# Four-layer block on one core: 23 expert tiles for 24, the last expert's constant row from DVE and one product, constant products moved and added on PE

## The reference

```
logits = _gelu(x @ rw1) @ rw2
wgt, idx = jax.lax.top_k(jax.nn.softmax(logits, axis=-1), TOP_K)   # TOP_K = 2
for e in range(E):                                                 # E = 8
    Ye = _gelu(x @ w1[e] + b1[e]) @ w2[e] + b2[e]
    Ce = _gelu(b1[e]) @ w2[e] + b2[e]
    for k in range(TOP_K):
        mask = idx[..., k] == e
        active = jnp.any(mask).astype(x.dtype)
        out = out + active * wgt[..., k:k + 1] * jnp.where(mask[..., None], Ye, Ce)
```

## Time and profile before

| | us |
|---|---|
| median of 3 runs | 454.55 |
| the three runs | 454.42, 454.55, 456.42 |
| the profiled execution, its own time | 456.11 |
| its span, first to last instruction | 454.3 |
| PE busy | 387.2 (85%) |
| DVE busy | 343.7 (76%) |
| ACT busy | 294.3 (65%) |
| POOL busy | 93.0 (20%) |
| mean granted clock of PE | 0.931 |

### The profile page before, as it was taken

One profiled execution on the slowest core, in us unless ns is written; L12 is line 12 of the kernel. 1 busy time (PEld: TensorE's weight loads), 2 busy tenths in 40 slices (PEclk: granted clock), 3 DMA queues, 4 the chain that ended last, 5 costly groups with the idle time before them and its releaser, 6 DMA issues.

```text
span 454.3 us, 7376 instructions
## 1 busy us (share of the span) xinstructions
PE 387.2 (85%) x2617; PEld 336.5 (74%) x2628; DVE 343.7 (76%) x512; ACT 294.3 (65%) x518; POOL 93.0 (20%) x103
## 2 busy tenths in 40 slices
PE   3999665699883489999999999999999988898866
PEld 3998643477762379999999999999995876777523
DVE  5999969789465999999999913980014587989995
ACT  5996784478885277675766767676542555776754
POOL 3000002000030142332536322456430000000000
PEclk9999869699896589999999999999998899999989
DMA  7600000000057615711161486550006000000001
GB/s 286 203 1 1 2 0 0 0 1 1 0 185 272 207 47 181 248 49 35 36 221 37 156 282 234 161 209 27 14 23 198 0 1 0 2 12 25 1 25 35
DMA packets 22757, 38.82 MB, mean 85 GB/s; under 512 B 2089, under 2 KB 17082, under 8 KB 22594
## 3 DMA queue, kind: packets, MB, share of 16 engines
q1 hardware_dynamic: 17634, 25.50, 16.9%
q0 software_dynamic: 2624, 7.34, 4.9%
q10 hardware_dynamic: 2464, 5.51, 3.3%
HBM read 33.10 MB, written 5.24 MB: 84 GB/s over the span
## 4 chain that ended last, share of the span: by engine, by line
PE 58%; DVE 23%; issue 9%; ACT 8%; DMA 1%; POOL 1%; POOLq 0%; SPq 0%; ACTq 0%; DVEq 0%
PE bank L1559 19%; PE bank L1538 18%; PE bank L1398 3%; PE bank L1369 2%; PE bank L1429 2%; DVE scr L830 2%; DVE scr L832 2%; PE bank L1620 2%; PE bank L1530 1%; PE bank L1610 1%; PE bank L1416 1%; PE bank L1587 1%; DMA v<-in_kT 1%; POOL small L368 1%; DVE big L1196 1%
## 5 line engine op out<-in xcount | busy, mean ns | idle before, releaser
L1538 PE MATMUL bank<-big,yT 128*128 x384 | 86.7, 379 | 0.0
L611 ACT ACTIVATE yT<-bank,big 128x128 f32<-128x128 f32 x192 | 54.7, 368 | 46.9 <-PE bank L1559 46.8
L1538 PEld LDWEIGHTS bank<-big,yT 128*128 128x128 f32 x384 | 71.2, 190 | 8.7
L401 POOL DMA_INDIRECT xg<-token_rows,rowi x24 | 37.1, 1545 | 60.2 <-PE bank L1530 35.7
L368 POOL TENSOR_TENSOR small<-small 128x2 f32<-128x2 f32 (+1 forms) x9 | 10.1, 1117 | 191.3 <-DVE small L1216 85.7
L416 POOL DMA_INDIRECT choice_rows<-yo,rowo x24 | 28.2, 1174 | 64.2 <-ACT yo L620 48.8
L1369 PE MATMUL bank<-identf,scr 128*128 128x128 f32 x240 | 31.5, 292 | 3.8 <-DVE scr L843 3.8
L1369 PEld LDWEIGHTS bank<-identf,scr 128*128 128x128 f32 x240 | 30.7, 209 | 4.1 <-DVE scr L843 4.0
L1559 PEld LDWEIGHTS bank<-ygT,w3T 128*128 128x128 f32 x256 | 30.8, 198 | 1.0 <-issue 0.6
L1559 PEld LDWEIGHTS bank<-ygT,big 128*128 128x128 f32 x256 | 29.8, 192 | 1.9 <-issue 1.6
L1559 PE MATMUL bank<-ygT,big 128*128 128x128 f32 x256 | 29.9, 275 | 1.4 <-ACT ygT L603 1.4
(11 more groups left out here) (353 smaller groups left out, 831.3 us busy)
## 6 DMA issues: line engine op xcount, KB each, us to landing
big<-in_moe_w SPq DMA_DIRECT2D x16, 1024.0 KB
v<-in_kT SPq DMA_DIRECT2D x2, 512.0 KB, 4.5
big<-in_gateT SPq DMA_DIRECT2D x1, 1024.0 KB, 7.0
big<-in_upT SPq DMA_DIRECT2D x1, 1024.0 KB, 9.0
big<-in_downT SPq DMA_DIRECT2D x1, 1024.0 KB, 11.5
x<-in_x_bsc SPq DMA_DIRECT2D x1, 1024.0 KB, 13.8
token_rows<-y POOLq DMA_DIRECT2D x4, 256.0 KB, 7.4
ek<-in_w3a ACTq DMA_DIRECT2D x1, 1024.0 KB
```

The lines of the kernel that those rows point to most:

```text
L401: gp.indirect_dma_start(out=xg[:, j % 3], out_offset=None, in_=Y1, in_offset=bass.IndirectOffsetOnAxis(ap=rowi[:, j:j + 1], axis=0)).then_ ...
L611: ins = sc.activation(hT[j % 2][:, c], ps[1 + 2 * (j % 2) + c // 4][:, (c % 4) * P:(c % 4 + 1) * P], ACT.Gelu, bias=b1s[:, c, j:j + 1])
L1538: ins = te.matmul(ps[5 + 2 * (j % 2)][:, 0:C], hT[j % 2][:, c], big[:, bass.ds(at + (W2_AT + c * C), C)], start=(c == 0), stop=(c == IC - 1))
```

## The change

- `TILES` is 23. The last expert (7) gets no slot of zeros: it has ceil(n/128) tiles (`last_e[:, 2]` in `nti`, `last_e[:, 1]` in `tbase`), its scattered row 0 is no constant row, and 2048 rows and 7 zero rows fit into 23 tiles.
- Its constant row is made apart: an extra column of `of_tile` turns its `b1` along with the others, ACT applies gelu to it (`last_g`, 128 x 8), DVE sums gelu times the second weights over the 8 chunks (`last_w2`, 8 instructions on 128 x 256, behind `l2_int`), one product of PE with a matrix that picks row 7 sums over partitions, ACT copies that out ahead of its last `store_yo`, and SP moves the one row into `cb` ahead of the load of the other seven.
- Of the constant products the first 8 become 7, the 9 behind `x_to_channels` are spread as 4, 4 and 2 between the `bias` pairs, and 6 are added ahead of `down_l2(p, 0)` from the second group on and 9 ahead of `turn_l3(5)`. The wait for `x_l2` goes ahead of the 6.

```diff
@@ -34,7 +34,7 @@
-    TILES = (2 * NT + E) // P + E
+    TILES = 2 * NT // P + E - 1
@@ -187,14 +187,18 @@
-        of_tile = sb("of_tile", [P, TILES])
+        of_tile = sb("of_tile", [P, TILES + 1])
+        last_e = sb("last_e", [P, 3, E])
+        last_w2 = sb("last_w2", [P, C])
+        last_g = sb("last_g", [P, IC])
...
@@ -303,9 +307,11 @@
+            sp.wait_ge(s["last_row"], 1)
+            sp.dma_start(cb[E - 1:E, :], last_w2[E - 1:E, :]).then_inc(s["ld_cb"], 16)
             for b in range(2):
-                sp.wait_ge(yg_stored[b], 16 * (TILES // 2))
-            sp.dma_start(cb[0:E, :], YT[1 + 2 * NT:1 + 2 * NT + E, :]).then_inc(s["ld_cb"], 16)
+                sp.wait_ge(yg_stored[b], 16 * ((TILES + 1 - b) // 2))
+            sp.dma_start(cb[0:E - 1, :], YT[1 + 2 * NT:2 * NT + E, :]).then_inc(s["ld_cb"], 16)
...
@@ -407,7 +413,7 @@
-                            pool.wait_ge(ld_xg[b], 16 * (TILES // 3))
+                            pool.wait_ge(ld_xg[b], 16 * ((TILES + 2 - b) // 3))
...
@@ -623,6 +629,7 @@
             copy_w1(1)
+            sc.activation(last_g[:], b1s[:, :, TILES], ACT.Gelu).then_inc(s["last_gelu"], 1)
             def load_w3():
@@ -658,6 +665,8 @@
+            act.wait_ge(s["last_ps"], 1)
+            sc.activation(last_w2[0:E, :], ps[6][0:E, 0:C], ACT.Copy).then_inc(s["last_row"], 1)
             store_yo(TILES - 1)
...
@@ -1037,6 +1046,10 @@
+            ve.tensor_scalar(of_tile[:, TILES:TILES + 1], iota_p[:, 0:1], float(E - 1), None, ALU.is_equal)
+            link(ve.tensor_scalar(last_e[:, 0], iota_e, float(E - 1), None, ALU.is_equal))
+            ve.tensor_scalar(last_e[:, 1], last_e[:, 0], -1.0, 1.0, ALU.mult, ALU.add)
+            link(ve.tensor_scalar(last_e[:, 2], last_e[:, 0], -1.0 / 256, 0.5 + 1.0 / 512, ALU.mult, ALU.add))
             dve.wait_ge(s["logits"], 1)
...
@@ -1064,12 +1077,12 @@
-            link(ve.tensor_scalar(nti, incl.rearrange("p (e t) -> p e t", t=T)[:, :, T - 1], 1.0 / P, 0.5 + 1.0 / 512, ALU.mult, ALU.add))
+            link(ve.scalar_tensor_tensor(nti, incl.rearrange("p (e t) -> p e t", t=T)[:, :, T - 1], 1.0 / P, last_e[:, 2], ALU.mult, ALU.add))
             link(ve.tensor_scalar(nti, nti, MAGIC, MAGIC, ALU.add, ALU.subtract))
             link(ve.tensor_tensor_scan(tend, onesf[:, 0:E], nti, 0.0, ALU.mult, ALU.add))
             link(ve.tensor_tensor(tbase, tend, nti, ALU.subtract))
-            link(ve.tensor_scalar(tbase, tbase, float(P), None, ALU.mult))
-            link(ve.scalar_tensor_tensor(slot, offs, 1.0, tbase.unsqueeze(2).to_broadcast([P, E, T]), ALU.add, ALU.add))
+            link(ve.scalar_tensor_tensor(tbase, tbase, float(P), last_e[:, 1], ALU.mult, ALU.add))
+            link(ve.tensor_tensor(slot, offs, tbase.unsqueeze(2).to_broadcast([P, E, T]), ALU.add))
...
-            ve.tensor_scalar(of_tile[:], te_[:, 0], iota_p[:, 0:1], None, ALU.is_equal)
+            ve.tensor_scalar(of_tile[:, 0:TILES], te_[:, 0], iota_p[:, 0:1], None, ALU.is_equal)
...
+            link(ve.scalar_tensor_tensor(row_c[:, 0], te_[:, 0], float(E - 1), row_c[:, 0], ALU.is_lt, ALU.mult))
             link(ve.tensor_tensor(row_c[:, 2], row_c[:, 0], row_c[:, 1], ALU.mult))
...
@@ -1151,6 +1165,17 @@
             ve.tensor_tensor(qd, qd, sdrow.unsqueeze(1).to_broadcast([P, HC2, C]), ALU.mult).then_inc(s["l2_int"], 1)
+
+            dve.wait_ge(s["last_gelu"], 1)
+            dve.wait_ge(s["ld_w"], 32 * E)
+            for c in range(IC):
+                at = (E - 1) % RING * EW + W2_AT + c * C
+                if c == 0:
+                    ins = ve.tensor_scalar(last_w2[:], big[:, at:at + C], last_g[:, c:c + 1], None, ALU.mult)
+                else:
+                    link(ins)
+                    ins = ve.scalar_tensor_tensor(last_w2[:], big[:, at:at + C], last_g[:, c:c + 1], last_w2[:], ALU.mult, ALU.add)
+            ins.then_inc(s["last_sum"], 1)
...
@@ -1542,7 +1567,7 @@
             for c in range(IC):
-                ins = te.matmul(ps[5][:, c * TILES:(c + 1) * TILES], b1r[:, c * P:(c + 1) * P], of_tile[0:E, :], start=True, stop=True)
+                ins = te.matmul(ps[5][:, c * (TILES + 1):(c + 1) * (TILES + 1)], b1r[:, c * P:(c + 1) * P], of_tile[0:E, :], start=True, stop=True)
             ins.then_inc(s["b1_turned"], 1)
...
@@ -1567,6 +1592,8 @@
                 before = at
+            pe.wait_ge(s["last_sum"], 1)
+            te.matmul(ps[6][0:E, 0:C], last_e[:, 0], last_w2[:], start=True, stop=True).then_inc(s["last_ps"], 1)
             down_tile(TILES - 1, before)
             transpose_w3(pe, te)
...
@@ -1577,9 +1604,9 @@
-            keep_clock(6, 8)
+            keep_clock(6, 7)
             pe.wait_ge(s["ld_b2"], 16)
-            pe.wait_ge(s["ld_cb"], 16)
+            pe.wait_ge(s["ld_cb"], 32)
...
@@ -1613,9 +1640,10 @@
             def down_l2(p, t):
+                if p >= 1 and t == 0:
+                    pe.wait_ge(s["x_l2"], p)
+                    keep_clock(3, 6)
                 pe.wait_ge(s["h2_ready"], HP2 * (p + 1))
-                if p >= 1:
-                    pe.wait_ge(s["x_l2"], p)
                 for c in range(HC2):
...
@@ -1682,11 +1710,15 @@
-            for p in range(G):
-                bias(p)
+            bias(0)
+            keep_clock(6, 4)
+            bias(1)
+            keep_clock(6, 4)
             x_to_channels(0)
+            keep_clock(6, 2)
+            bias(2)
+            bias(3)
             pe.wait_ge(s["l2_int"], 1)
-            keep_clock(6, 9)
             for p in range(G + 2):
...
@@ -1722,6 +1754,8 @@
                 elif p >= 2:
+                    if p == G:
+                        keep_clock(0, 9)
                     turn_l3(2 * p - 3)
                 if 1 <= p <= G:
                     up_l3(2 * p - 1)
```

More of the change, by code:

```diff
@@ L597, in _ @@
             act.wait_ge(s["b1_turned"], 1)
-            sc.activation(b1s, ps[5][:, 0:IC * TILES].rearrange("p (c j) -> p c j", c=IC), ACT.Copy).then_inc(s["b1s_ready"], 1)
+            sc.activation(b1s, ps[5][:, 0:IC * (TILES + 1)].rearrange("p (c j) -> p c j", c=IC), ACT.Copy).then_inc(s["b1s_ready"], 1)
             def copy_xT(j):
```

13 lines of the change are left out of this document (7 added, 6 removed).

## The result

The changed kernel took **444.59 us** (median of 4 runs, 443.08 to 445.26), the kernel before, run beside it, 455.18 (median of 4, 454.42 to 456.42): a ratio of 0.9758, 95% interval 0.9738 to 0.9779. The forecast was 443.0 with a range of 441.5 to 447.8, and faster with a chance of 0.97. The profiled execution took 445.26 (span 443.4, mean granted clock 0.950), where that of before took 456.11 (454.3, 0.931). So the spans differ by 10.9 us and the medians by 10.6, for a forecast sum of 11.55.

What follows compares the result with a forecast made beforehand. PE alone bounds the expert loop; in the groups the chain changes engines, with DVE nearly full and PE sometimes at half clock. -7.25 + 0.1 - 2.1 - 1.6 + 0.3 - 1.0 = -11.55 from 454.55 gives 443.0, range 441.5 to 447.8.

Steps and rivals of the forecast that it cites:

- Rival D: Expert loop's end: set by something that stays, such as the scatters; at worst 2.5 us lost, 445.5; chance 0.03.
- Head: Start of the groups: spread constants keep the full clock, L1610 starts 2.2 us earlier; net -2.1 with the product's +0.43.
- 8 x 0.216 + 8 x 0.21 = 3.4: Groups' head: PE's time in us for bias(0), 4 constants, bias(1), 4 constants at the full clock.
- Six constants: Ahead of L1620: third group keeps the clock, -1.6 us (ends 0 and -1.77); fourth group, where they don't fit, +0.3.
- Nine constants: Ahead of turn_l3(5): full clock near the end, about 1.1 us less PE time; -1.0, ends 0 and -1.2.
- The product: PE's one f32 product for the last expert's row, ahead of the last tile's down products: +0.43 us on the chain.
- 16 us in hand: DVE's eight sum instructions end at about 311.8, PE needs them at 327.7, so waiting for them costs 0.
- three hidden costs: ACT's extra copy (some 0.4 us), the row's own transfer and ACT's extra gelu (0 to 0.3): each taken as 0.
- 0 to +0.25: Routing: L1083 may slow with rows of 23 two-byte elements, every second starting mid-word; +0.1 us taken.
- A: Clock falls anyway, there or elsewhere: 448.2 if all three falls stay, 444.1 to 445.1 if one; chance 0.32.
- B: DVE bounds the groups, so an earlier PE only meets a busy DVE: only -6.7 us, 447.8; chance 0.09.
- C: A late last_sum stops PE, which works in order, at the last tile; slower than before past 339.3; chance 0.01.

Runs made afterwards that it cites:

- The tile alone: Changed kernel with every constant product of PE put back as in the kernel before: 449.55 us, 0.9864 of the kernel before.
- the three constants: Changed kernel with 3 constant products in place of 8 ahead of the last turn (turn_last): 444.96 us, 0.9763 of the kernel before.
- the product elsewhere: Changed kernel with the last expert's product moved behind the turns of w3, DVE copying the row into cb: 443.85 us, 0.9741 of the kernel before.
- the constants alone: Kernel before, with 24 tiles, with only the constant products placed as in the changed kernel: 452.04 us, 0.9908 of the kernel before.
- the bare sum: Changed kernel, but DVE starts the last expert's sum only after tile 21's down products: 450.51 us, 0.991 of the kernel before.
- all three edits: Changed kernel with product behind L272, 3 constants for 8 ahead of turn_last, and 28 constants in layer 0: 443.33 us, 0.9726 of the kernel before.

## Why the prediction was right

**The bound and the tile** stood as forecast. The tile alone gives 6.5, where the forecast was -7.25 + 0.1 + 0.43 for the product, so -6.72; the loop has 23 tiles at the old pace. Rival D is refuted by it: the loop's end is PE's, and the last scatter (333.36) now waits for ACT's rows, not for the scatter before. Only the profile of the three constants shows a path from that scatter ending last, for 0.38.

**The constants** give 4.0 alone; forecast were 2.4 for the head behind the bias' start, 1.6 and 1.0, less 0.3, so 4.7. Every one but the fourth group's of these terms has the right sign and place:

- Head: 2.20 by the table for 2.4. The part that failed is "8 x 0.216 + 8 x 0.21 = 3.4": the alternating blocks took 4.05. 0.216 was the price of the down products, and a bias product costs 0.24 even in a row of eight; the rest is that I had taken the prices of long runs of one kind for blocks of four.
- Six constants: -1.69 in the profiled pair for -1.6, and +0.07 in the fourth group for +0.3: there they hold L1648 by 0.2 (it starts at 405.25, DVE's L1221 had ended at 405.02), and behind it PE waits 1.12 for DVE ahead of L1682, as it did before. The term is right for an execution that has one fall without them, and the kernel before was profiled in one; that the pair agrees so well is in part luck. On the average the times put it at 0.8, loosely.
- Nine constants: 0.55 for 1.0. The step "about 1.1 less; DVE's idle 1.22 behind the gelu is the upper bound" took DVE's idle time for what could be gained, and it was not the bound. DVE does use nearly all of its 1.22: its last reduction is 11.44 earlier (444.62 to 433.18), 1.17 more than the fourth group's end. But PE's turn L1682 at 433.21 needs DVE's L1297, which ends just before this reduction starts, and it had only 0.48 in hand: in the kernel before L1272 had ended at 443.40 and PE came at 443.88. Now PE idles 1.10 there, and the chain from 424.46 to 433.16 has DVE alone. The eight constants ahead of the last turn stand behind that and take no part in the loss (from L1693 to L1711 3.87, and 3.98 before the change), but they hold the first half of the last row, quantised at 436.49, until 437.66; with three of them it is 3.37.
- The product: 0.53 where 0.43 was written, and the down products behind it took 0.19 more than before. With the product elsewhere they did not.

The forecast sum was 11.55, the spans differ by 10.9. By the table, what is missing is 0.16 ahead of tile 22, 0.23 up to the bias, 0.20 in the head and 0.45 at the end; 0.08 more than forecast came in the second and third group, 0.23 in the fourth and 0.08 behind the start of the last products. That makes 0.65.

**The base.** 443.0 was the sum taken from 454.55. The nine runs of the changed kernel have a mean of 444.5, and the kernel before has batch medians from 454.56 to 456.08: its 37 single times lie at 454.2 to 454.8 or above 455.6, with none between. The sum was made from an execution at 456.11 and set against a median of three that lay at the lower of these. Of the 1.59 between 443.0 and 444.59, 0.65 is the sum's by the spans; the other 0.94 come from this base, whose median beside the changed kernel was 455.18, and from medians of few runs. The mistake is in calling 1.56 "the spread of runs" and taking it off, when the terms were read in the slower execution.

**Covers.** DVE's "16 us in hand" were 11: the sum ended at 316.65 and PE came at 328.0. The cover held, and the run without it shows what it is worth, 6 to 7 us, where I had written 4.2. The three hidden costs that I set at 0 (ACT's copy, the row's transfer, the gelu) showed nothing in the chain. The routing's "0 to +0.25" for the rows of 23 was 0.

**The rivals.** A did not happen in the profiled pair: the granted clock is 1.00 from 165 us on. But its mechanism is real and I had it half right. (Its "if one stays, 444.1 to 445.1" was added wrongly: by the same terms the head alone would leave 445.6 and the nine alone 444.0.) Whether a gap of 2 us brings the clock down differs between executions of nearly the same code (one of two in the kernel before and with the tile alone, two of two without the six constants). By the Trainium skill (TensorE: Matmul & The Clock Gate, Part 1), whose rule is that the gate counts on its own time and not from the kernel's start, this is what should be seen; the runs agree with it, though none shows the count. Only the changed kernel was profiled twice, with no fall in the groups in either. The filled gaps, 0.69 to 0.74 long, had no fall behind them in any of the ten profiles that have the six constants. B is refuted as a whole by the constants alone, and right for the last rows, where DVE now ends last. The prediction also missed a wait of DVE for gelu: 2.05 us ahead of L1257 at 382.71, in the second group, behind products at the full clock. It is there unchanged (374.05), so such a wait is no sign of a slow clock by itself. C needs a late sum; the bare sum shows the mechanism, its price, and how far the change is from it.

**The 0.26 ahead of tile 22** is the first tile's. Its first products start 0.07 earlier than before (160.84 for 160.91) and take 5.27 for 4.94, since the clock comes back later: 0.52 for 0.67 in the window from 162 to 164. They took 5.21 with 24 tiles and only the constants changed, and 4.75 to 5.28 in the kernels with 23. So the price is the clock's, and none of the change is shown in it.

**Not settled.** The start of one and the same group of L1449's products, late in layer 0, lies anywhere from 123.71 to 125.81 in the profiles of the changed kernel and of its variants whose code is the same up to there; what sets it was not found. Why the down products behind the product took 0.19 more was not tried apart. And nothing was run with the constant blocks of the head ordered as one block per kind.

## What to carry to other kernels

When a stall is filled, write down which wait ends last once it is gone, and how much that one has in hand: half of the gain at the end was lost to a result of DVE that had been 0.48 us ahead of need. The idle time of the other engine elsewhere is no bound. Cost short runs of alternating products from rows where they alternate. Where a gap of PE is followed by a fall of the clock in some executions and not in others, a single profile shows either nothing or the whole amount, so look at several profiles and at all single times. And take the terms and the base of a sum from the same execution.

## What was not expected of the hardware

**DVE beside POOL.** Six scalings of DVE on 128 x 256 (L1165) took 5.26 us in the changed kernel and 1.81 in the kernel before. One tile less moves POOL's cast and subtraction from 311.05 and 312.39 to 305.90 and 307.24, onto them. The answer for that source line gives shortest, median and longest of its instructions in ns, then the first and last start:

```profile
L1165 DVE TENSOR_SCALAR scr<-scr,small x6: 368/373/2780, 304.7 to 307.2; 128x256 f32<-128x256 int32 x6
```

The median is 0.37, and the last one starts at 307.2, as POOL's subtraction of 2.61 does, and took 2.78. The fifth starts at 305.91, beside POOL's cast of 1.25, and took some 1.3. The sum's last instruction met the next cast of 1.25 (315.12) and took 1.43 for 0.485. In the run with all three edits DVE came 2.5 us earlier; the six took 1.66, and the sum met the subtraction instead, which starts at 306.87 there:

```profile
L1174 DVE SCALAR_TENSOR_TENSOR last_w<-big,last_g,last_w x7: 484/485/2802, 307.0 to 312.4; 128x256 f32<-128x256 f32 x7
```

and in the run of the bare sum, where POOL computed nothing beside it:

```profile
L1178 DVE SCALAR_TENSOR_TENSOR last_w<-big,last_g,last_w x7: 485/485/486, 326.2 to 329.4; 128x256 f32<-128x256 f32 x7
```

Beside the subtraction one took 2.80, and the last one 1.43, beside a cast at 312.30; the others keep 0.485, and so do all seven in the run of the bare sum. By the Trainium skill (SBUF — State Buffer, Who interferes with whom) the two engines share one pair of ports, and whichever of two such instructions starts first holds it to its end while the other stands still. One instruction of DVE stretched to about the end of POOL's, each time they met, agrees with that, and where DVE had started first, at 303.92 in the run with all three edits, it was POOL's cast that took 1.84 for 1.25; a sharing of bandwidth would have stretched several by less. The stretching cost the total nothing here only because the sum has its 11 us.

**Rows of odd length.** 368 elements of 2 bytes in rows of 23 took 0.31, as 384 in rows of 24 did. The slower form, for which the Trainium skill (VectorE: DVE Perf Modes, Mode 2×_1P) gave a reason by asking for 16-bit data at 4-byte alignment for packed reads, did not appear. This doesn't refute the page: as the prediction says, its full rule for one source needs no packing, and no run tells which of the two ways this instruction took. The price stands with the measured 0.31.

**The spread has a place.** From the group of L1449 at 125.50, near the end of layer 0, to the end of the span, the two profiles of the changed kernel took 317.90 and 318.04. What differs between executions lies mostly ahead of it. In the earliest, the bare sum's (123.71), four products took 1.04 at 66.63 that took 1.89 at 68.35 in the changed kernel. The rest lies in the first tile, and, where gaps of 2 us are left, in the groups.
